# One core, one layer of log-polar pooling and convolution: the second half's weight preparation goes from VectorE to accumulating transfers

## The reference, cut to what matters

```python
masks = _logpolar_masks()                  # 12 masks of 9x9, each a mean over its bin
xp = log_pooling(x)                        # x: (32, 256, 28, 28) -> 12 pooled planes per channel
out = conv(xp, w_conv1, stride=(4, 3))     # 12 taps of 256x256
out = out + conv(x, w_center) + b_center   # a 13th tap
mean, var = out.mean((0, 2, 3)), out.var((0, 2, 3))
return relu((out - mean) * rsqrt(var + 1e-5) * gamma + beta + x)
```

## Time and profile before

| what | value |
| --- | --- |
| median of three runs | 1605.91 us (1605.81 to 1606.45) |
| profiled execution, its own time | 1605.88 us |
| span in that profile | 1604.1 us |
| PE busy | 1458.2 us, 91% |
| DVE busy | 1474.4 us, 92% |
| ACT busy | 760.6 us, 47% |
| POOL busy | 122.6 us, 8% |

### The profile page before, as it was taken

The page is one execution under the profiler, slowest core; times in us unless marked ns, Lnnn a source line. Parts: engine busy times, 40 slices in busy tenths (PEclk is TensorE's granted clock), DMA queues, the critical chain, the costliest instruction groups (busy, mean ns, idle before and its releaser), DMA issues.

```text
span 1604.1 us, 22797 instructions
## 1 busy us (share of the span) xinstructions
PE 1458.2 (91%) x8518; PEld 1456.1 (91%) x8518; DVE 1474.4 (92%) x1512; ACT 760.6 (47%) x853; POOL 122.6 (8%) x155
## 2 busy tenths in 40 slices
PE   9899999999999999999999999999999999995000
PEld 9899999999999999999999999999999999995000
DVE  8999999999999999999999999999999999996731
ACT  4345555445444554445444554445444554444632
POOL 1000000000000000000000000000000000000100
PEclk9999999999999999999999999999999999998555
DMA  6244443344333443344333443344334444569999
GB/s 170 69 80 88 84 94 81 80 94 84 81 80 74 85 93 81 80 94 84 81 80 74 87 92 82 80 94 84 83 79 77 87 89 103 155 198 380 419 425 398
DMA packets 46632, 197.55 MB, mean 123 GB/s; under 512 B 5536, under 2 KB 5536, under 8 KB 46624
## 3 DMA queue, kind: packets, MB, share of 16 engines
q0 software_dynamic: 20736, 82.45, 28.4%
q1 hardware_dynamic: 21024, 89.32, 15.2%
q10 hardware_dynamic: 4864, 25.69, 3.9%
HBM read 147.67 MB, written 49.77 MB: 123 GB/s over the span
## 4 chain that ended last, share of the span: by engine, by line
PE 86%; DVE 4%; ACT 4%; ACTq 3%; issue 1%; DMA 0%; DVEq 0%
PE acc L772 29%; PE acc L774 29%; PE acc L773 29%; ACTq L509 3%; ACT phase L506 2%; ACT phase_rest L506 2%; DVE phase_rest L514 1%; DVE pooled_split L515 1%; DVE d L514 0%; DVE inner_split L515 0%; DVE y_stage L514 0%; ACT unread L451 0%; ACT x_pad L506 0%; DMA x_pad<-x 0%; ACT w_inner L392 0%
## 5 line engine op out<-in xcount | busy, mean ns | idle before, releaser
L418 ACT ACTIVATE pooled_split<-phase_rest 128x1456 fp32r<-128x1456 f32 x192 | 273.0, 1422 | 595.5 <-DVE phase_rest L514 595.5
L515 DVE TENSOR_TENSOR pooled_split<-phase_rest,pooled_split 128x1456 fp32r<-128x1456 f32 x192 | 317.8, 1669 | 0.0
L772 PE MATMUL acc<-pooled_split,w_first_outer 128*128 128x364 f32 x768 | 253.8, 330 | 1.1 <-DVE pooled_split L515 1.1
L772 PE MATMUL acc<-pooled_split,w_outer 128*128 128x364 f32 x768 | 252.2, 328 | 1.5 <-DVE pooled_split L515 1.4
L774 PE MATMUL acc<-pooled_split,w_outer 128*128 128x364 f32 x768 | 252.7, 329 | 0.0
L773 PE MATMUL acc<-pooled_split,w_first_outer 128*128 128x364 f32 x768 | 252.5, 329 | 0.0
L773 PE MATMUL acc<-pooled_split,w_outer 128*128 128x364 f32 x768 | 252.5, 329 | 0.0
L774 PE MATMUL acc<-pooled_split,w_first_outer 128*128 128x364 f32 x768 | 252.3, 328 | 0.0
L772 PE MATMUL acc<-inner_split,w_inner 128*128 128x392 f32 (+1 forms) x640 | 215.8, 337 | 2.9 <-DVE w_inner L557 2.9
L772 PE MATMUL acc<-inner_split,w_first 128*128 128x392 f32 (+1 forms) x640 | 216.8, 339 | 0.2 <-DVE inner_split L515 0.2
L773 PE MATMUL acc<-inner_split,w_inner 128*128 128x392 f32 (+1 forms) x640 | 216.6, 338 | 0.0
(11 more groups left out here) (95 smaller groups left out, 2486.1 us busy)
## 6 DMA issues: line engine op xcount, KB each, us to landing
row<-x_wide POOLq DMA_DIRECT2D x64, 558.0 KB, 5.8
ends<-x_wide POOLq DMA_DIRECT2D x64, 504.0 KB, 5.5
x_pad<-x SPq DMA_DIRECT2D x64, 392.0 KB, 3.1
y_dram<-y_stage SPq DMA_DIRECT2D x30, 784.0 KB, 3.3
out<-phase ACTq DMA_DIRECT2D x16, 784.0 KB, 28.4
phase<-y_dram SPq DMA_DIRECT2D x15, 784.0 KB, 16.7
phase_rest<-y_dram SPq DMA_DIRECT2D x14, 784.0 KB, 14.1
out<-phase_rest ACTq DMA_DIRECT2D x14, 784.0 KB, 30.0
```

Source lines behind the costliest of these rows:

```text
L418: nc.scalar.activation(view(pooled_split, 2 * j * PAIR, (1, PAIR)), reused_view(POOLED_LOW + 2 * j * PAIR, (1, PAIR)), ACT.Copy)\
L515: sub = lambda out_, a, b: nc.vector.tensor_tensor(out_, a, b, ALU.subtract)
L772: nc.tensor.matmul(place, hi_w, hi_in, start=start, stop=False)
```

## The change

Only the second half (c = 1) of the weights in image 0 is touched, and two small clearings.

- A new input `w_side` brings three planes for each partition, laid out so that copy + add + add gives the three sides of half 1. POOL's `sum_weights` issues a chain of five transfers of 128x768 into `spare`: one copy, two that add `w_side`, two that add the mid planes of `w_raw`. Each waits until the one before it has landed (`w_plus_ready`). The chain stands in POOL's queue behind the two transfers of half 0 and ahead of the `row2` and `ends` transfers of half 1.
- DVE's `transform_weights(1)` becomes one wait for all five (80 counts of the semaphore) and one instruction of 128x768, sum - 4 mid.
- The low halves of groups 5 and 6 of half 1 leave DVE. ACT's `begin_outer_weights` writes the high half, the whole scaled value into `spare`, and minus the high half; POOL's `low_outer_weights` adds the whole onto it with a transfer inside SBUF. Group 5 is done by ACT ahead of `split_inner(1)`, group 6 behind the inner groups. TensorE waits for those landings ahead of pairs 0 and 1 of half 1.
- The first clearing of the edges of `d03` and of `row3v` goes from DVE to POOL's start; `ZEROED` is 9 instead of 7.

```diff
+            def sum_weights():
+                parts = [w_side[:, k, :] for k in range(3)]
+                parts += 2 * [w_raw[:, 1, RAW_MID:RAW_MID + 3, :].rearrange("p k o -> p (k o)")]
+                pool.dma_start(w_sums(1, 0, 3), parts[0]).then_inc(w_plus_ready, 16)
+                for k in range(1, len(parts)):
+                    wait_first(w_plus_ready, 16 * k)
+                    pool.dma_start(w_sums(1, 0, 3), parts[k], accum_op=ALU.add).then_inc(w_plus_ready, 16)
+
+            def low_outer_weights():
+                for g in range(INNER_GROUPS, len(GROUPS)):
+                    high, low, whole = outer_weights(g)
+                    wait_first(w_outer_begun, g - INNER_GROUPS + 1)
+                    pool.dma_start(low.bitcast(F32), whole, accum_op=ALU.add).then_inc(w_outer_lo_ready[g - INNER_GROUPS], 16)
...
+                    if isinstance(image, int):
+                        (sum_weights, low_outer_weights)[c]()
...
+            def begin_outer_weights(g):
+                a, b, raw, factor = GROUPS[g]
+                high, low, whole = outer_weights(g)
+                source = view(w_stage, (RAW + raw) * CHANNELS, (1, (b - a) * CHANNELS))
+                act.wait_ge(w_loaded[1][1], 16)
+                nc.scalar.activation(high, source, ACT.Copy, scale=factor).then_inc(w_outer_hi_ready, 1)
+                nc.scalar.activation(whole, source, ACT.Copy, scale=factor)
+                act.wait_ge(w_outer_hi_ready, g - INNER_GROUPS + 1)
+                nc.scalar.activation(low, high.bitcast(F32), ACT.Copy, scale=-1.0).then_inc(w_outer_begun, 1)
...
+                    if first and c == 1:
+                        begin_outer_weights(INNER_GROUPS)
                     split_inner(s)
...
-                        split_weights(c, range(len(GROUPS)))
+                        split_weights(c, range(len(GROUPS) if c == 0 else INNER_GROUPS))
                         act.wait_ge(warmed_up, 1)
+                    if first and c == 1:
+                        begin_outer_weights(INNER_GROUPS + 1)
...
                 dve.wait_ge(w_loaded[c][0], 16)
-                wait_from_one(dve, w_lo_ready, len(GROUPS) * c)
+                if c == 1:
+                    dve.wait_ge(w_plus_ready, 5 * 16)
+                    nc.vector.scalar_tensor_tensor(out=w_sums(1, 3, 3), in0=raw(RAW_MID, 3), scalar=-4.0,
+                                                   in1=w_sums(1, 0, 3), op0=ALU.mult, op1=ALU.add)\
+                        .then_inc(w_sums_ready, 1)
+                    return
...
-                    lo_of_weights(c, [FIRST_OUTER_GROUP - 1])
+                    if c == 0:
+                        lo_of_weights(c, [FIRST_OUTER_GROUP - 1])
                     lo_of_pooled(c, 0)
                     third_sum(c)
-                    lo_of_weights(c, range(FIRST_OUTER_GROUP, len(GROUPS)))
+                    if c == 0:
+                        lo_of_weights(c, range(FIRST_OUTER_GROUP, len(GROUPS)))
...
-                        pe.wait_ge(w_lo_ready, c * len(GROUPS) + min(FIRST_OUTER_GROUP + j, len(GROUPS)))
+                        if c == 0:
+                            pe.wait_ge(w_lo_ready, min(FIRST_OUTER_GROUP + j, len(GROUPS)))
+                        elif j < 2:
+                            pe.wait_ge(w_outer_lo_ready[j], 16)
```

More of the change, by code:

```diff
@@ L5, with conv_bn_relu_program @@
 from concourse import mybir
-def conv_bn_relu_program(nc, x, x_wide, w_raw, b_center, gamma, beta, out, y_dram):
+def conv_bn_relu_program(nc, x, x_wide, w_raw, w_side, b_center, gamma, beta, out, y_dram):
     F32 = mybir.dt.float32
@@ L132, in row3v, with d_edges, row3v_edges @@
             return reused_view(start_of["pooled_split"] + ROW3V_AT + first, *dims)
+        def d_edges():
+            return view(d03, 0, (TALL, 2 * U), (TALL - 1, 2))
+        def row3v_edges():
+            return row3v(-ROW3V_AT, (ROW3V_H, W + 3), (1, EDGES))
         def w_part(c, lo, tap):
@@ L138, in w_part, with w_sums, outer_weights @@
             return (w_first_outer, w_outer)[c], (lo * (TAPS - INNER_TAPS) + tap - INNER_TAPS) * CHANNELS
+        def w_sums(c, first, n):
+            return view((y_stage, spare)[c], first * CHANNELS, (1, n * CHANNELS))
+        ALL_LO = len(GROUPS) + INNER_GROUPS
+        def outer_weights(g):
+            a, b = (t - INNER_TAPS for t in GROUPS[g][:2])
+            n = (1, (b - a) * CHANNELS)
+            return (view(w_outer, a * CHANNELS, n),
+                    view(w_outer, (TAPS - INNER_TAPS + a) * CHANNELS, n),
+                    view(spare, (6 + a) * CHANNELS, n))
         LAST = IMAGES - 1
@@ L199, in conv_bn_relu_program @@
         w_loaded = [[sem(f"w_loaded{c}{part}") for part in range(2)] for c in range(CH)]
+        w_plus_ready = sem("w_plus_ready")
         w_sums_ready = sem("w_sums_ready")
@@ L203, in conv_bn_relu_program @@
         w_lo_ready = sem("w_lo_ready")
+        w_outer_hi_ready = sem("w_outer_hi_ready")
+        w_outer_begun = sem("w_outer_begun")
+        w_outer_lo_ready = [sem(f"w_outer_lo_ready{k}") for k in range(2)]
         zeroed = sem("zeroed")
@@ L254, in conv_bn_relu_program @@
         block = ctx.enter_context(nc.Block())
-        ZEROED = 7
+        ZEROED = 9
         @block.gpsimd
@@ L261, in _ @@
             for edge in (std[:, :], pooled_split[:, 2 * PAIR:2 * PAIR + HALF], row2[:, :], ends[:, :],
-                         x_pad[:, 0:2 * H], x_pad[:, X_PAD:X_PAD + 2 * H], x_pad[:, CH * X_PAD:]):
+                         x_pad[:, 0:2 * H], x_pad[:, X_PAD:X_PAD + 2 * H], x_pad[:, CH * X_PAD:], d_edges(), row3v_edges()):
                 if edge.dtype == F32R:
@@ L349, in _ @@
             image_steps(LAST - 2)
-            sp.wait_ge(w_lo_ready, CH * len(GROUPS))
+            sp.wait_ge(w_lo_ready, ALL_LO)
+            for k in range(2):
+                sp.wait_ge(w_outer_lo_ready[k], 16)
             sp.wait_ge(y_saved, 16 * (LAST - 3))
@@ L386, in split_weights @@
                         act.wait_ge(w_sums_ready, c + 1)
-                        source = view(y_stage, 0, (1, (b - a) * CHANNELS))
+                        source = w_sums(c, 0, b - a)
                     else:
@@ L430, in copy_middle @@
                 if isinstance(image, int) and image == 0:
-                    act.wait_ge(w_lo_ready, CH * len(GROUPS))
+                    act.wait_ge(w_lo_ready, ALL_LO)
                 for m in range(2):
@@ L537, in transform_weights @@
                                                op0=ALU.mult, op1=ALU.add).then_inc(w_moved, 1)
-                dve.wait_ge(w_moved, 2 * c + 1)
+                dve.wait_ge(w_moved, 1)
                 nc.vector.scalar_tensor_tensor(out=view(y_stage, 0, (1, 3 * CHANNELS)), in0=raw(RAW_MID, 3),
@@ L541, in transform_weights @@
                     .then_inc(w_moved, 1)
-                dve.wait_ge(w_moved, 2 * c + 2)
+                dve.wait_ge(w_moved, 2)
                 nc.vector.scalar_tensor_tensor(out=side(0, 3), in0=raw(RAW_MID, 3), scalar=-2.0,
@@ L614, in differences @@
                 wait_from_one(dve, pooled_ready, PAIRS * s)
-                nc.vector.memset(view(d03, 0, (TALL, 2 * U), (TALL - 1, 2)), 0.0)
+                if not (isinstance(image, int) and s == 0):
+                    nc.vector.memset(d_edges(), 0.0)
                 sub(view(d03, 1, (U * TALL, 2), (TALL, U), (1, H)),
@@ L644, in three_columns @@
                 wait_from_one(dve, pooled_done, PAIRS * s - PAIRS + 1)
-                nc.vector.memset(row3v(-ROW3V_AT, (ROW3V_H, W + 3), (1, EDGES)), 0.0)
+                if not (isinstance(image, int) and s == 0):
+                    nc.vector.memset(row3v_edges(), 0.0)
                 dve.wait_ge(inner_lo_ready, 2 * s + 2)
@@ L845 @@
     w_raw = np.ascontiguousarray(w[:, order][:, :, by_half].reshape(128, halves, len(order), channels))
+    a, c, d, f = (w_raw[:, 1, k] for k in range(4))
+    w_side = np.stack([np.concatenate(part, axis=1) for part in ((d, d, a), (f, a, c), (f, np.zeros_like(a), c))], axis=1)
     def per_partition(v):
@@ L857 @@
         "w_raw": w_raw,
+        "w_side": np.ascontiguousarray(w_side),
         "b_center": per_partition(L0_conv_b_center),
```

## The result

| | before | after |
| --- | --- | --- |
| median of 15 runs | 1606.39 us (1605.81 to 1607.27) | 1609.66 us (1608.66 to 1610.61) |
| profiled execution, its span | 1604.1 | 1608.3 |

The ratio is 1.0020 with an interval of 1.0013 to 1.0026: 3.3 us slower, 2.1 to 4.2. The forecast of 1605.5 and its range up to 1608.2 missed it; the median lies nearest to rival 2 (1610.3), which had little chance.

What follows compares the result with a forecast made beforehand. It took DVE's lateness at 78 us as the bound: with L at 38.2, L - 36.9 - 1.74 gives -0.4; 1604.1 - 0.4 = 1603.7 of span, plus 1.78 around it, 1605.5 us; range 1603.3, with 0.1 for measurement, to 1608.2.

Steps and rivals of the forecast that it cites:

- rival 2: Image 0, half 1: chain lands at 41.5 and PE's clock falls, +4.4, 1610.3; chance 0.16 of more than +1.5.
- the 1.74 us of the low outer weights: DVE, half 1: groups 5 (0.60 us) and 6 (1.14 us) leave its queue, a gain of 1.74 us.
- the ACT limit: Group 0's high half must wait for ACT's `split_inner(1)`, so the gain is at most 2.6 us.
- the outer transfers behind the chain stay hidden: POOL's queue after the chain: `row2`, `ends`, groups 5 and 6 land with 3 us or more to spare.
- the formula: End of kernel moves by L - 38.6 us, never below -2.6; forecast -0.4 us.
- L: Landing time of the chain's fifth transfer, forecast at 38.2 us, 3.3 us after DVE stands ready.
- sharing with SP's loads: Chain's second transfer: about 1.0 us extra beside plain loads, bounds nothing to 2.2, landing at 22.3.
- the copy landed: Chain's first transfer: issued at about 7.1, SP's loads taking half the engines, landing at 16.0 (15.0 to 16.5).
- the last three links: Chain's third to fifth transfers: 4.8 us each from issue to landing, bounds 4.2 and 5.5.
- the four hand-overs: POOL, between a landing and the next issue: 0.5 us each, bounds 0.2 and 0.6.
- The pause: PE before half 1 in image 0: some 4.1 us instead of 3, clock counted as held at 1.00.
- the cover: PE's later waits of 2.65 us shrink by 1.74, leaving 0.9 us to absorb slow matmuls.

Runs made afterwards that it cites:

- e1: Changed kernel without the chain of five transfers, DVE making half 1's weight sums with its five instructions as before; 1604.53 us.
- e2: Changed kernel with a chain of three transfers (the three sides), DVE adding the mid planes with two instructions; 1603.60 us.
- e8: Changed kernel with the second to fifth transfers of the chain held until SyncE's last load has landed; 1611.84 us.
- e9: Changed kernel with a chain of four transfers, the second `w_side` plane never added, so the sums lack a plane; 1603.25 us.
- e3: Changed kernel with SyncE's two loads of half 1's weights held until the chain's second transfer has landed; 1608.58 us.
- e6: Changed kernel with the low halves of groups 5 and 6 of half 1 back on DVE, the chain of five kept; 1610.80 us.
- e4: Changed kernel with image 0 written out for PE and 90 short filler matmuls in PE's pause before half 1; 1609.68 us.
- e5: Changed kernel with image 0 written out for PE and 60 short filler matmuls in PE's pause before half 1; 1608.81 us.
- e7: Kernel with the chain of three transfers, and half 1's weight sums moved ahead of its differences on DVE; 1603.80 us.

## Why the prediction was wrong

**What held.** The bound of the kernel, DVE's lateness at 78 us and not PE's idle time; the 1.74 us of the low outer weights (1.75 in the changed kernel's trace, 1.55 in e1's, 1.8 in e1's median); the ACT limit of -2.6 (e2: -2.7); that `row2`, `ends` and the outer transfers behind the chain stay hidden; and the formula, end moves by L - 38.6, never below -2.6. With the measured landings it gives +3.5 for 42.1 (measured +3.3), +6.5 for e8's 45.1 (measured +5.5; the interval reaches 7.9) and -2.5 for e9's 36.1 (measured -3.2). That 3.5 and 3.3 lie so close is in part luck: the formula leaves out the clock's 0.4 to 0.5 us and has DVE 0.2 later than it was (group 0 at L + 2.7, not L + 2.8), and the profiled execution shows 3.7.

**The step that failed** is one term of the sum for L: "Second: issue 16.5, 4.8, and about 1.0 for sharing with SP's loads (nothing to 2.2 ...)". It took 9.6, 3.8 more than the 5.8 of that sum; against the 5.0 to 5.1 of a link on free engines the loads cost it 4.5, twice the upper bound. The bound came from `ends` of half 0, 7.7 us, read as sharing with SP's loads. The trace of before has something else: in it SyncE's queue moves its first packet at 13.0 us, when 6.6 of the 7.7 were over. What `ends` shared the engines with was `row2`, ahead of it in its own queue. So the row priced the wrong thing.

The profile counts each queue's packets, megabytes and share of the 16 engines' time. q0 is GpSimd's, q1 SyncE's. In order: the changed kernel from 15.62, the issue of the second link, to 19.8; from 19.8 to 24.8; the third link alone, 27.3 to 30.6; e3 from 22.77, the issue of its slow third link, to 27.1; and before, 11.6 to 12.95:

```profile
q1 hardware_dynamic: 365, 1.70, 101.9%
q8 instruction: 1, 0.02, 1.5%
...
q1 hardware_dynamic: 659, 0.98, 56.6%
q0 software_dynamic: 144, 0.39, 40.9%
...
q0 software_dynamic: 144, 0.39, 80.1%
...
q1 hardware_dynamic: 203, 1.28, 91.1%
...
q0 software_dynamic: 71, 0.29, 106.7%
```

For 4.2 us after its issue the second link moves nothing, while 1.70 MB of plain loads pass; its first packet starts at 19.84. On free engines the third link's starts 1.6 us after its issue (27.38). That is 2.6 us of the 4.5. Then it shares with the loads, and its packets take 4.9 us instead of 3.1, which is nearly all of the rest. In e3 the slow link again moves nothing for 4.4 us. e3 and e8 show that the loads are the cause of at least 3 of the 4.5 us, the 8.1 of e3's third link against 5.1, and the queues' rows show the two parts. Why the first packet comes so late stays open, and so does the share of the one packet of q8, which stands at 18.6 here (see the last section).

**The other terms**: the copy landed 1.0 us earlier than summed (15.0, not 16.0), the last three links took 5.0, 5.1 and 5.0 instead of 4.8, 0.7 together, and the four hand-overs nearly 0.6 each instead of 0.5, 0.3 together. 3.8 - 1.0 + 0.7 + 0.3 = 3.8, and L's error is 42.1 - 38.2 = 3.9. The loads did not take half of the engines from the copy: in the changed kernel SyncE's queue moves its first packet at 13.95, 2.3 us after its issue, and GpSimd's, with `row2`, `ends` and the copy, its last of these at 14.7.

**The clock.** The pause was 7.9 us and not 4.1; the clock fell in it, and the end moved from DVE's 3.3 to PE's 3.7. Rival 2 had priced the lower level for 4.7 us and 1.5 us past its cover; it lasted from about 42 to 52 us, of which 5.6 us had matmuls in them. These cost PE 2.6 us, yet little came through, for the cover was 2.1 and not 0.9. The prediction took 2.65 for PE's later waits, as the profile counts them from the modelled end of a matmul; but matmuls in a row start 0.17 apart and last 0.33, and counted from start to start PE loses 3.8 in those waits. Less the 1.75 of the two groups, that is 2.1. Rival 2's 1610.3 lies near the median by luck: its links, hand-over included, were 6.0 instead of 5.6, its second one was more than 2 us too short, and its clock 1 us too dear.

**The chances.** 3.8 us of the error come from one term with one row behind it, used with a bound too narrow. The estimate of 2.9 us for 384 KB, worked out from the formula of the Trainium skill ("DMA: Bandwidth & Descriptors", "Anatomy of one DMA"), is out too: on free engines the links took 4.8 to 5.1 in the changed kernel and e8.

## What to carry to other kernels

A chain of dependent transfers is priced link by link, each with its whole latency (here 5.6 us for 384 KB that add, hand-over included), and with the state of the engines at the moment of its issue: here a transfer issued behind megabytes of another queue's plain loads moved nothing until 1.7 MB of them had passed. A row in which a transfer is slow says nothing of its price beside loads until one has looked which queue was at work in it. Move only as many links off the busy engine as land before it needs them: three were free, four nearly so, the fifth cost 6.4 us. And when an engine's lateness is what counts, test the two halves of such a change alone; here one was worth 1.8 us and the other hid it.

## What was not expected of the hardware

- A transfer issued behind another queue's backlog did not share the engines from the start here: its first packet came 4.2 us after its issue (changed kernel) and 4.4 (e3's third link), against 1.6 on free engines (changed kernel and e8), and 1.6 too for e3's second link, which was issued when the loads had only 1.9 us to run.
- The fifth link took 5.0 to 5.2 us in the changed kernel, e3, e6 and e8, but 6.4 in e4 and 6.3 in e5, and the second link of e3 took 6.4 with no load beside it for most of its time. In each of these three a packet of 16 KB of queue q8, of the kind that the profile calls instruction, stands within the link's flight and lasts 0.9 to 1.0 us (at 41.1, 40.9 and 17.6 us), and in none of the links of 4.6 to 5.4 us is there one. That one such packet on one engine holds up the whole link is a guess that no run tests. The rows of e4 from 36.79 to 43.2 and of e3 from 15.79 to 22.2:

```profile
q8 instruction: 1, 0.02, 0.9%
...
q8 instruction: 1, 0.02, 1.0%
```

- The granted clock did not follow the length of PE's pause alone. It stayed at 1.00 through pauses of 2.94 us (before) and 2.95 (e1), yet in e2 it fell about 1.5 us after PE had resumed from a pause of 2.06, and was back before 46; in e9 it stayed at 1.00 after a pause of 2.05. In e5 it fell 1.4 us after a pause of 1.85, and in e7 within a pause of 2.60. What decides it stays open. The window of e2, and then PE's row and a window of e9:

```profile
42.40:45.60 3.20, 3.20 (x12) 3.20 (x11) 3.13 (x6) 0.57 (x1) 0.87 (x1) 0.50 0.26 43
...
40.78 0.44 PE L840 MATMUL acc<-inner_split,w_inner 128*128 128x392 f32 x1 [2.05 <-DVE w_inner L621]
...
41.00:60.00 19.00, 18.25 (x106) 17.93 (x106) 18.86 (x22) 9.18 (x10) 2.61 (x3) 1.00 0.56 101
```

- 17 matmuls at the lower level set PE back by 2.6 us and cost the kernel 0.4 to 0.5, since PE had waits behind them that they filled.
- Matmuls of 120 columns stood 0.11 us apart at the full clock (90 in 10.0 us), where those of 364 to 392 stand 0.17 to 0.18.
